# Recurrent layer of a two-layer language model: chunks outside and heads inside, weights kept in DRAM as half-precision pairs, GpSimd's two operations moved to VectorE

## The reference

```python
h = attention_only_layers(x)                 # "tower": 4 layers of single-head causal attention
h = h + rwkv(layernorm(h))                   # recurrent layer, the one that is changed
h = h + ffn(layernorm(h))                    # ternary weights, GELU
h = h + moba(layernorm(h))                   # block attention, 16 heads
h = h + glu(layernorm(h))                    # weights are looked up in a table of 16 values
```

```python
xx = previous token of x (zero for the first)
xk, xv, xr = x * mix + xx * (1 - mix)        # one mix vector each for k, v, r
r = sigmoid(xr @ Wr.T); k = xk @ Wk.T; v = xv @ Wv.T
kv = k * v;  w = exp(-exp(time_decay))
out_t = (state_t + u * kv_t) * r_t;  state_{t+1} = state_t * w + kv_t
return out @ Wo.T
```

## Time and profile before

| what | value |
|---|---|
| three runs | 2750.97, 2754.61, 2758.75 us, median 2754.61 |
| the profiled execution | 2755.32 us, its span 2753.3 us |
| PE busy | 2423.6 us, 88% of the span |
| DVE busy | 1825.1 us, 66% |
| ACT busy | 778.3 us, 28% |
| POOL busy | 512.6 us, 19% |
| granted PE clock, mean | 0.947 |
| chain that ended last | PE 54%, DVE 29%, issue 10%, ACT 4% |

### The profile page before, as it was taken

One profiled execution on the slowest core, in us unless ns is written; L12 is line 12 of the kernel. 1 busy time (PEld: TensorE's weight loads), 2 busy tenths in 40 slices (PEclk: granted clock), 3 DMA queues, 4 the chain that ended last, 5 costly groups with the idle time before them and its releaser, 6 DMA issues.

```text
span 2753.3 us, 35040 instructions
## 1 busy us (share of the span) xinstructions
PE 2423.6 (88%) x12786; PEld 1217.6 (44%) x12786; DVE 1825.1 (66%) x3279; ACT 778.3 (28%) x1695; POOL 512.6 (19%) x308
## 2 busy tenths in 40 slices
PE   4899349989999999689878999899899999889999
PEld 2555224434444444334334555455455455344444
DVE  7655887989999999856574444544544555677722
ACT  3555432111111111233313333333333333211111
POOL 4000122233323333213440000300300100300000
PEclk8999769999999999899989999999999999899999
DMA  2001000111111110101210000100100000100001
GB/s 98 31 30 44 33 15 31 35 49 48 31 36 48 49 33 32 42 37 46 76 46 16 1 1 1 62 1 2 62 1 1 16 31 1 50 1 1 1 1 61
DMA packets 25897, 82.91 MB, mean 30 GB/s; under 512 B 2944, under 2 KB 15488, under 8 KB 18688
## 3 DMA queue, kind: packets, MB, share of 16 engines
q1 hardware_dynamic: 25728, 80.67, 8.6%
HBM read 70.17 MB, written 10.49 MB: 29 GB/s over the span
## 4 chain that ended last, share of the span: by engine, by line
PE 54%; DVE 29%; issue 10%; ACT 4%; POOL 1%; DVEq 1%; DMA 0%; ACTq 0%; SPq 0%; POOLq 0%
PE ps L226 13%; PE ps L443 8%; PE ps L983 6%; DVE work L607 6%; PE ps L836 6%; PE ps L823 6%; DVE work L625 3%; PE ps L732 3%; PE ps L528 3%; DVE work L576 3%; DVE h L448 2%; PE ps L241 2%; PE ps L857 2%; PE ps L250 2%; DVE work L571 1%
## 5 line engine op out<-in xcount | busy, mean ns | idle before, releaser
L528 PE MATMUL ps<-planes,wa 128*128 128x512 f16 x2304 | 510.7, 381 | 24.3 <-DVE work L571 22.1
L528 PEld LDWEIGHTS ps<-planes,wa 128*128 128x128 f16 x2304 | 226.0, 98 | 299.8 <-issue 31.4
L443 PE MATMUL ps<-wa,work 128*128 128x512 f16 x1216 | 291.4, 394 | 55.8 <-POOL work L698 39.8
L226 PE MATMUL ps<-planes,wa 128*128 128x512 f16 x1152 | 271.6, 384 | 23.9 <-DVE planes L1442 16.3
L448 DVE TENSOR_TENSOR h<-ps,h 128x512 f32<-128x512 f32 x240 | 158.7, 685 | 92.7 <-PE ps L443 92.5
L443 PEld LDWEIGHTS ps<-wa,work 128*128 128x128 f16 x1216 | 120.4, 101 | 216.9 <-issue 67.4
L557 ACT ACTIVATE work<-work 128x512 f16<-128x512 f32 x64 | 40.3, 630 | 567.7 <-POOL work L696 567.7
L226 PE MATMUL ps<-planes 128*128 128x512 f16 x768 | 186.5, 387 | 4.5 <-issue 4.5
L607 DVE TENSOR_SCALAR work<-work,lutx,par 128x256 int32<-128x256 int32 x384 | 189.8, 563 | 0.0
L226 PEld LDWEIGHTS ps<-planes,wa 128*128 128x128 f16 (+1 forms) x1152 | 111.6, 99 | 152.4 <-DVE planes L1442 16.3
L696 POOL TENSOR_TENSOR work<-work 128x512 f32<-128x512 f32 x64 | 81.4, 1271 | 442.0 <-DVE work L582 442.0
(11 more groups left out here) (153 smaller groups left out, 4078.4 us busy)
## 6 DMA issues: line engine op xcount, KB each, us to landing
stg<-in_ff_w SPq DMA_DIRECT2D x16, 1024.0 KB, 4.8
stg<-in_rw_w SPq DMA_DIRECT2D x16, 1024.0 KB, 4.9
stg<-in_mo_w SPq DMA_DIRECT2D x16, 1024.0 KB, 4.8
work<-in_glu_idx SPq DMA_DIRECT2D x48, 128.0 KB, 2.1
glu_dec<-work SPq DMA_DIRECT2D x48, 128.0 KB, 1.7
stg<-glu_dec SPq DMA_DIRECT2D x6, 1024.0 KB, 4.8
out<-h SPq DMA_DIRECT2D x4, 1024.0 KB, 4.2
planes<-in_glu_idx SPq DMA_DIRECT2D x1, 2304.0 KB, 7.9
```

The lines of the kernel that those rows point to most:

```text
L226: mm = te.matmul(ps[:, bank, :], w(i, kt), x(j, kt), start=(kt == 0 and n == 0), stop=(kt == KT - 1 and n == 2))
L443: mm = te.matmul(ps[:, bank, :], x, y, start=(m == 0), stop=(m == len(pairs) - 1))
L528: mm = te.matmul(ps[:, 3 * m + what, :], rw_w(slot, what, i, kt, m), mix[what][j][:, kt, c * CH:c * CH + CH], start=(kt == 0 and z == 0), ...
```

## The change

- The recurrence runs over chunks outside and heads inside, written out without a loop. A head's output for four tiles goes into banks 4 to 7 and stays there for all 16 heads; `rw_dve_acc` adds to `h` once for each chunk (16 additions in place of 128). R, K and V have one set of banks (0 to 2).
- Every head needs its weights again in every chunk. So all 16 pieces are split once, during the tower: high half on ScalarE (`rw_split_act`), low half on GpSimd in four parts (`rw_split_pool`), the pair stored to `rw16` in DRAM. 32 loads of 2 MB (two heads, all four weights) bring them back into four slots: two in `wa`, two in the middle columns of planes 2 to 5.
- LN and mix of chunks 1 to 3 move from the tower's end into the recurrence (heads 2 to 11 of the chunk before). LN of the feed-forward stage's chunks 0 to 2 stands in chunk 3's heads. They use one bank, 3.
- VectorE multiplies by the receptance and makes the low half of the head before; GpSimd does neither.
- 40 decode blocks stay in the recurrence, 8 stand in the first eight feed-forward steps. The first four ternary pieces (two groups) are made during chunk 3, where two were.

The core of the diff:

```diff
+        rw16 = nc.dram_tensor("rw16", (P, RW_PIECES, 2 * PW), F16, kind="Internal").ap()
+RW_SLOT = [q % 4 for q in range(RW_UNITS - 4)] + [0, 2, 3, 0]
         def ln_bank(e):
-            return ps[:, (6 if e < 16 else 4) + e % 2, :]
+            if 4 <= e < 28:
+                return ps[:, 3, :]
+            return ps[:, (6 if e < 4 else 4) + e % 2, :]
+        def rw_pe_proj(pe, c, n):
+            q, m, t = c * R_GROUPS + n // RG, n % RG, c * HEADS + n
+            if m == 0:
+                pe.wait_ge(rw_in[RW_SLOT[q]], 16 * rw_uses(q))
+            for what, done, free in ((0, r_ps, r_sb), (1, k2_ps, k_sb), (2, v_ps, kv_sb)):
+                if t > 0:
+                    pe.wait_ge(free, t)
...
+        def rw_pe_out(pe, c, n):
+            pe.wait_ge(o_lo, t + 1)
+            if n == 0 and c > 0:
+                pe.wait_ge(rw_acc, TPC * c)
+            for j in range(TPC):
+                for z, (x, y) in enumerate(PASSES):
+                    mm = te.matmul(ps[:, 4 + j, :], oT[t % 4][x][:, j * P:j * P + P], rw_wo(q, y, m),
+                                   start=(n == 0 and z == 0), stop=(n == HEADS - 1 and z == 2))
+        def rw_pe(pe):
+            for c in range(NC):
+                for n in range(HEADS):
+                    rw_pe_proj(pe, c, n)
+                    if c < NC - 1 and 4 <= n < 4 + TPC:
+                        ln_pe(pe, 0, c + 1, n - 4)
+                    if c == NC - 1 and n >= 4:
+                        ln_pe(pe, 1, (n - 4) // TPC, (n - 4) % TPC)
+                    if c > 0 or n >= 2:
+                        rw_pe_out(pe, *divmod(c * HEADS + n - 2, HEADS))
+        def rw_act(act, c, n):
...
+        def rw_dve(dve, c, n):
...
+            if t > 0:
+                rw_dve_lo(dve, t - 1)
...
+            ve.tensor_tensor(o_buf, o_buf, r_buf, ALU.mult).then_inc(o32_sb, 1)
+        def rw_dve_lo(dve, t):
+            dve.wait_ge(o_hi, t + 1)
+            ve.tensor_tensor(oT[t % 4][1], o_buf, oT[t % 4][0], ALU.subtract).then_inc(o_lo, 1)
+        RW_DEC = [(0, 1, 4, 5, 6, 7, 12, 13, 14, 15), (0, 3, 4, 5, 6, 7, 12, 13, 14, 15),
+                  (0, 3, 4, 5, 6, 7, 12, 13, 14, 15), (0, 1, 4, 6, 7, 9, 10, 12, 13, 15)]
+        def rw_dve_all(dve, chain):
+            for c in range(NC):
+                for n in range(HEADS):
+                    rw_dve(dve, c, n)
+                    if n == 1 and c > 0:
+                        rw_dve_acc(dve, c - 1)
+                    if c < NC - 1:
+                        if n == 2:
+                            ln_dve_chunk(dve, 0, c + 1, chain)
+                        if n == 3:
+                            ln_chunk(dve, ln_dve_x, 0, c + 1)
+                        if 8 <= n < 8 + KT:
+                            mix_dve(dve, c + 1, n - 8)
+                    else:
+                        if n in (2, 5, 9):
+                            f1 = (2, 5, 9).index(n)
+                            dve.wait_ge(rw_acc, TPC * (f1 + 1))
+                            ln_dve_chunk(dve, 1, f1, chain)
+                        if n >= 4:
+                            ln_dve_lo(dve, 1, (n - 4) // TPC, (n - 4) % TPC)
+                        if 3 <= n < 15:
+                            ln_dve_x(dve, 1, (n - 3) // TPC, (n - 3) % TPC)
+                    if n in RW_DEC[c]:
+                        dec_block(dve, i)
...
-        def rw_pool(pool, p, s):
-                ge.tensor_tensor(o_buf, o_buf, r_buf, ALU.mult).then_inc(o32_sb, 1)
-                ge.tensor_tensor(oT[s % 2][m][1], o_buf, oT[s % 2][m][0], ALU.subtract).then_inc(o_lo, 1)
...
+        MIX_AT = [(), (0,), (1,), (2, 3)]
+        def rw_split_act(act, l, c):
+            act.wait_ge(stg_full[0], l * 64 + 16 * (P_RW + c + 1))
+            act.wait_ge(rw_stored[k], l * 32 + 16 * (c // 2 + 1))
+            se.activation(half_, stg[:, 0, :], ACT.Copy).then_inc(rw_hi, 1)
...
+            for j in range(RW_PIECES):
+                sp.wait_ge(rw_lo, j + 1)
+                sp.dma_start(rw16[:, j, :], wa[:, j % 2 * 2 * PW:(j % 2 + 1) * 2 * PW]).then_inc(rw_stored[j % 2], 16)
+                if j < RW_PIECES - 1:
+                    load_rw32(j + 1)
...
+            rw_pe(pe)
+            pe.wait_ge(ln_done, 28)
+            ff_pe_proj(pe, 0, 0)
+            rw_pe_out(pe, NC - 1, HEADS - 2), rw_pe_out(pe, NC - 1, HEADS - 1)
...
                     ff_dve_acc(dve, p, s)
-                    if s == 2:
-                        with first_pair(dve, p):
-                            dec_block(dve, RW_PAIRS - 1, rw_block(7, 0))
+                    with first_pair(dve, p):
+                        dec_block(dve, DEC_BLOCKS - FF_DEC + s)
```

More of the change, by code:

```diff
@@ L405, in ln_pe @@
             if e >= 2:
[L406 removed]
+                pe.wait_ge(ln_done, e if 4 <= e < 28 else e - 1)
             for kt in range(KT):
@@ L512, in __exit__ @@
                     self.inner.__exit__(*e)
[L515 to L525, removed]
+        def rw_pe_proj(pe, c, n):
+            q, m, t = c * R_GROUPS + n // RG, n % RG, c * HEADS + n
+            if n == 0:
+                pe.wait_ge(mix_lo, 12 * (c + 1))
+            if m == 0:
+                pe.wait_ge(rw_in[RW_SLOT[q]], 16 * rw_uses(q))
+            at = chunk_at(c)
+            for what, done, free in ((0, r_ps, r_sb), (1, k2_ps, k_sb), (2, v_ps, kv_sb)):
+                if t > 0:
+                    pe.wait_ge(free, t)
@@ L526, in rw_pe_proj @@
                 for kt in range(KT):
                     for z, (i, j) in enumerate(PASSES):
-                        mm = te.matmul(ps[:, 3 * m + what, :], rw_w(slot, what, i, kt, m),
-                                       mix[what][j][:, kt, c * CH:c * CH + CH], start=(kt == 0 and z == 0),
-                                       stop=(kt == KT - 1 and z == 2))
+                        mm = te.matmul(ps[:, what, :], rw_w(q, what, i, kt, m), mix[what][j][:, kt, at:at + CH],
+                                       start=(kt == 0 and z == 0), stop=(kt == KT - 1 and z == 2))
@@ new lines, in build @@
+        FF_DEC = 8
+        assert sum(map(len, RW_DEC)) + FF_DEC == DEC_BLOCKS
+        def rw_dve_all(dve, chain):
+            i = 0
+            for c in range(NC):
+                for n in range(HEADS):
+                    rw_dve(dve, c, n)
[19 more added lines that the diff above has]
+                        dec_block(dve, i)
+                        i += 1
@@ new lines, in _ @@
+            sp.wait_ge(mix_lo, 12)
+            sp.wait_ge(wsum_ps, 1)
+            load_idx(0)
+            load_rw(3)
+            i, q = 0, 4
+            for c in range(NC):
+                for n in range(HEADS):
+                    if q < RW_UNITS:
+                        before = max(x for x in range(q) if RW_SLOT[x] == RW_SLOT[q])
+                        if RG * before + RG + 1 <= c * HEADS + n:
+                            load_rw(q)
+                            q += 1
+                    if n in RW_DEC[c]:
+                        store_dec(i)
+                        i += 1
+                    if c == NC - 1 and n < 2:
+                        if n == 0:
+                            sp.wait_ge(mix_lo, 12 * NC)
+                        load_ff(n)
+                    if c == NC - 1 and n in (8, 10):
+                        sp.wait_ge(w_ready, WR_FF + n // 2 - 3)
+                        load_ff(n // 2 - 2)
@@ new lines, in _ @@
+            assert q == RW_UNITS
+            sp.wait_ge(rw_out, HEADS * NC)
+            sp.dma_start(b2row, a["b2"].rearrange("p (k t) -> p k t", k=2)).then_inc(b2_in, 16)
+            for k in range(4, 8):
+                sp.wait_ge(w_ready, WR_FF + k - 1)
+                load_ff(k)
+                for x in range(2 if k < 6 else 0):
+                    store_dec(i)
+                    i += 1
+                if k == 5:
+                    while i < DEC_BLOCKS:
+                        store_dec(i)
+                        i += 1
```

526 lines of the change are left out of this document (238 added, 288 removed).

## The result

The changed kernel takes 2684.84 us, median of 4 runs (2675.96 to 2685.69), against 2754.22 for the kernel before in the same comparison: a ratio of 0.974, 95% interval 0.9715 to 0.9764. In a second comparison it took 2680.91 us (2679.23 to 2684.02, 5 runs; ratio 0.973, 0.9717 to 0.9743). It is faster by 2.6 to 2.7%. The forecast was 2677.0 us (2632 to 2724).

The account below looks back on a forecast made before the run. It took LN and mix ahead of the recurrence, then VectorE stretched by GpSimd, as the bound. First head 340 + 2.7 + 657.9 + 13.2 + 14 = 1027.8, feed-forward 310: 1337.8, 78.2 us off 2755.3, so 2677 (2632 to 2724).

Parts of the forecast that it names:

- First head at 340: Entry: mix ends at 323, last low half at 329, store and load 9.7 us, tower 1; ends 328 to 352.
- The tower: Tower's 16 added ScalarE copies of 1.9 us mostly fit into idle time: 1 us in all, up to 32 without room.
- Recurrence, 687.8 us: First head to feed-forward: heads 10.36 us apart, 657.9, plus cold start 2.7, LN transposes 13.2, chunk 3 14.
- Chunk 3: Last recurrence chunk: VectorE 182 us against TensorE's 172, blocks bunching up; 14 us lost, between 0 and 35.
- Never stretched: The two operations moved to VectorE: by the rows GpSimd never stretches them; by the skill's rule 15 us more (2692).
- Feed-forward, 310 us: Feed-forward stage: 277 before, +3 entry, -4 earlier second weight group, +34 for decode blocks; ends 0 to 49 for the blocks.
- ternary pieces and clock: Feed-forward: about 7 us for ternary pieces and clock, on top of 27 for steps with decode blocks, making 34.
- After feed-forward: Behind the feed-forward stage: both kernels run the same code, so no change in time was taken.
- C: Rival, recurrence: one set of PSUM banks too few, TensorE waits in nearly every head with a block; 160 us, 2837; chance 0.07.
- A: Rival, chunk 3 and feed-forward: VectorE keeps up everywhere and the blocks hide; 2632; chance 0.15.
- B: Rival, tower and entry: ScalarE's copies or late loads hold each of 16 bodies 2 us; 32 us, 2709; chance 0.12.
- D: Rival, recurrence: weights come too late, a 2 MB load taking 26 us; 170 us, 2847; chance 0.02.

Follow-up runs that it names:

- e4: Changed kernel without VectorE's work for the 8 feed-forward decode blocks, whose stores go out with old data (only prices that work): 2627.05 us.
- e6: Changed kernel with 72 us of VectorE work put back, the multiply-add made three times in 12 of 16 heads: 2724.98 us, ratio 0.9895.
- e1: Changed kernel with the receptance multiply and the low half back on GpSimd: 2680.81 us, ratio 0.9732.
- e2: Kernel before with only the receptance multiply and low half moved to VectorE, low half behind the next head's product: 2825.48 us, ratio 1.0261.
- e5: As e2, but the low half stands behind its own multiply and the accumulations, ahead of the decode block: 2784.16 us, ratio 1.0106.
- e3: Changed kernel with the first head pair's weights asked for ahead of the last weight piece's store: 2674.95 us.
- e7: e1 with the same 72 us of VectorE work put back as in e6: 2743.73 us, ratio 0.997.
- e9: As e3, and the first decode block's indices asked for right behind those weights: 2663.31 us, ratio 0.968.
- e11: The changed kernel again, unaltered, as base of the second comparison: 2680.91 us, ratio 0.973.

## Why the prediction came out

It was right in sign and size, and for the most part by its own steps, but terms of it were off and cancelled, and one reason in it was wrong. By stage, measured less forecast: first head +5.6 us, recurrence +2.2, feed-forward -2.2, what follows -6.5. This is the profiled execution, the fastest; the medians lie 4 and 8 us above the 2677.

- *First head at 340*: 345.57. The mix ended at 330.0, not 323; store and load took 9.9 us, priced at 9.7 (the 2.3 us per MB there is 2.4 by the rows, as the sum uses it). The tower was 3.6 us late, not 1. It arose in the first bodies: waits of 5.89 and 1.77 us for VectorE where there were 2.23 and 1.29. No run isolated the tower's new copies. After that the bodies are 16.6 to 16.8 us apart, as before. The last layer was also costlier than priced: its third body took 16.4 us (291.88 to 308.32), not 12.07, with a wait of 3.68 for VectorE in it; the second took 19.6, near 14.83 + 4.
- *Recurrence, 687.8 us*: 690.0. Heads 10.36 us apart at a clock of 1.00 as forecast; one with a transpose 10.80, so 0.44 and not 0.55 for a transpose. Chunk 3 lost 16.5 us (177.2 for 15 heads, against 15 x 10.36 + 12 x 0.44 = 160.7), forecast 14.
- *"Never stretched"*: by rows of before I took the two moved operations to be out of GpSimd's reach. L640's longest in chunk 3 is 2262 ns, against 691. The Trainium skill (SBUF — State Buffer, Who interferes with whom, and the page's summary) said so: a VectorE instruction with two SBUF inputs contends with a GpSimd instruction that reads SBUF, and whoever comes second waits until the first has finished. The traces agree, down to a scan that waits out a split. But the 15 us that I worked out from it did not come: in chunk 3 one multiply of 16 (2.26 us) and two low halves of 16 (1.15 and 1.77) met a piece, 3.1 us in all.
- *Feed-forward, 310 us*: 307.8, by luck. Without the blocks it takes 256.4 us (e4). My sum has 276, in which before's own block stands with 5.5, so the base was 14 us too high. In part that is LN of two chunks, now in chunk 3: TensorE's waits ahead of transposes in this stage were 11.7 us before and are 4.2. The rest isn't split up. And the blocks cost 51, not 34 + 5.5. Most steps that I walked came to waits of 1.1 to 6.7 us, as forecast (1.8 to 8). The one with the longest wait, 13.19, stands at VectorE's loop edge, but there TensorE waits 7.28 us with no block too, in e4 and in the kernel before, so the block's part is 5.9. That wait in the kernel before, then in e4, then e4's stage:

```profile
1313.65 5.15 PE L443 MATMUL ps<-wa,work 128*128 128x512 f16 x16 [7.28 <-DVE h L448]
```
```profile
1190.74 6.01 PE L460 MATMUL ps<-wa,work 128*128 128x512 f16 x16 [7.28 <-DVE h L465]
```
```profile
1037.80:1294.20 256.40, 238.24 (x1064) 105.84 (x1064) 139.92 (x211) 87.03 (x133) 57.65 (x24) 0.96 0.14 47
```

What I had mis-sized is the 7 us for "ternary pieces and clock": the block beside two pieces cost a wait of 11.24 where such a step was to lose 1.8, and the same 1064 matmuls take 10.6 us longer than in e4 (248.87 against 238.24, clock 0.91 and 0.96). That is 20 us.
- *After feed-forward* I took the same time, 1337.3 us; it was 1330.8 with the same code, 2.4 of the difference being one idle "issue" instead of two. The rest is not explained. It goes with the new order: every kernel with it has 1330 to 1334 us there, every one with the old order 1337.
- *Rivals*. C (one set of banks) didn't come, and e6 shows how near it is: 18 us of added work a chunk cost TensorE 11 to 14. A failed in feed-forward. B came as 3.6 of its 32 us. D: loads landed in 7.5 to 7.9 us.

What the prediction had no view of is which part of the change matters. It credited the end of VectorE's stretching to the swap as well; e1 says that the swap gives nothing, and e2 and e5 that it would have cost 29 to 71 us without the other parts. What gains is the order, chunks outside and heads inside. It lets LN and mix of chunks 1 to 3 leave the entry, which is the 57 us read off the two timelines above; no run tested it by itself. And it takes 112 of 128 accumulations and the splits out of the recurrence: putting about as much VectorE work back costs e6 40 to 44 us, and without the splits the old order with the swap (e5) is 61 us faster. These prices don't add up to the 46 us of the recurrence, since each was taken with the rest of its kernel as it stood.

## What to carry to other kernels

When one engine's instructions hold up another's, price an operation that is moved between them by what it does to the queue behind it: the same swap was worth -71, -29, 0 and +19 us in four surroundings. Read an engine's slack from its waits for the bound engine, not from its busy share. When a stage is already dense, look at its two edges: here reordering two DMA requests and moving six blocks gave 56 us on top of the change's 69 to 74.

## What the runs showed of the hardware

- Beside GpSimd's one-input passes of 1.9 us VectorE's int16 operations of 0.23 us end with the pass (1.88), beside a two-input split of 4.4 us a predicated copy of 0.45 us took 3.69 (in e5). The accumulations out of PSUM kept their length: 673 to 693 ns for all 64 in feed-forward, where GpSimd was busy 55 us. The Trainium skill (SBUF — State Buffer, Who interferes with whom) leaves an instruction with one SBUF input outside the two-port modes out of the contention; the trace agrees.
- At the edge of VectorE's feed-forward loop there are 7.34 us of idle with no releaser, of which GpSimd's passes can cover the last 3.9. Such idle stands there in five other kernels that have a block just ahead of the edge: e1 6.51, e3 7.63, e7 5.94, e9 7.27, e11 7.68 us. In e4 it is 0.94 us, but the four b2 adds ahead of it take 6.97 us for 2.49 and the low halves behind it 8.24, and TensorE waits 7.28; in the kernel before these adds take 6.97 too. What the first 3.4 us are stays open; no run tested it.
